# A recurrent (GRU) layer: q's high part made by ScalarE in the first two blocks, and the update gate's products all ahead of the candidate's

## The chip, the cores and the metric

The kernel runs on one core of one Trainium2 chip. The metric is the time of one execution on the device, in microseconds (us). Three runs of the kernel before gave 1056.73 us in the median, between 1056.33 and 1056.75.

## What is computed

64 sequences of 128 steps pass through a GRU with 512 inputs and 512 hidden units, all in float32. Every fourth step a further dense layer is put on the state that goes on:

```
z = sigmoid([x_t, h] @ Wz + bz)
r = sigmoid([x_t, h] @ Wr + br)
h_cand = tanh([x_t, r * h] @ Wh + bh)
h_new  = (1 - z) * h + z * h_cand
h_next = tanh(h_new @ Wp + bp) if (t + 1) % 4 == 0 and t < 127 else h_new
out[t] = x_t + h_new
```

In this document R, Z and C are the gates r, z and h_cand, and q is r * h, the operand of C's recurrent product.

## The kernel before

**Precision.** A float32 operand is held as two float16 parts, `hi` (the rounded value) and `lo` (what is left), both scaled. A product of two such operands is three matmuls: weights hi with values hi, weights lo with values hi, weights hi with values lo. The state and q lie in `h_split` and `q_split`, [128, 4, 2, 64]: four row groups of 128 hidden units, hi and lo, 64 sequences. HALVES are row groups 0 and 1 (LOW on TensorE) and 2 and 3 (HIGH).

**Products with x.** They do not depend on the state and are made ahead, in blocks of 8 steps: block 1's while block 0 runs, and so on. Block 1's are plain matmuls of 512 columns (`fill`); blocks 2 to 14 go by a scheme with seven products (`stage`, matmuls of 256 columns), for which the sums of weight quarters are made in steps 2 to 14 (`make_wsum`, `split_wsum`) and sums of x beside them (`make_x_sum`, `split_slot`). TensorE works on these between the end of one step's C product and the start of the next step's R product, so that it has work while gates and state are made.

**One step t, by engine** (every engine runs its own queue strictly in the order written; they meet in semaphores):

- TensorE: R's 48 recurrent matmuls of 64 columns, the first part of Z's among the last of them; the rest of Z's; then C's 48, which read `q_split`. The last four of Z's matmuls (row group 3, values lo) stand between C's matmuls on q's high part and those on its low part. Then come the products with x of this step.
- ScalarE: the sigmoid of R in two halves (`squash`, L504), the high part of a weight sum (L465) and of sums of x (L458) where the step has them, the sigmoid of Z, the tanh of C in two halves, and then the copies that put x's share into the accumulators (`seed`, L524) and bring the products with x out of PSUM.
- VectorE: per half `q_split` hi <- gate R * h (L868), then per half `q_full` <- gate R * h in float32 (L870), then per half q's low part <- `q_full` - hi (L857); the low parts of the sums (L714, L706); `keep` (L883), `new` (L888), the new state's hi part (L898), the full state (L901), its low part (L857), the output (L909), and then sums and maxima of x for later blocks.

Steps 0 to 15 are the first two blocks, BLOCK being 8. Weights are still being prepared in step 0 to 3 (`split_rec`, L692 and L498; magnitudes, L628).

Of the kernel before, what the change touches and what calls it, by code (L numbers as in the profile page):

```python
# [5 lines left out]
ALU = mybir.AluOpType  # L6
# [10 lines left out]
BLOCK = 8  # L17
RING = 4
R, Z, C, PROP = range(4)
# [40 lines left out]
def gru_kernel(nc, x, h0, wz, wr, wh, wp, biases, out):  # L60
# [106 lines left out]
    with ExitStack() as ctx:  # L167
# [150 lines left out]
        def propagates(t):  # L318
            return t % CHUNK == CHUNK - 1 and t < T - 1

        def props_before(t):
            return t // CHUNK

# [100 lines left out]
        def _(act):  # L424
# [75 lines left out]
            def squash(g, func, count, halves):  # L500

                act.wait_ge(product_done[g], count + 1)
                for half in halves:
                    nc.scalar.activation(gate[g][:, half, :], acc[g][:, half, :], func, scale=unscale[:, g:g + 1]).then_inc(gate_ready[g], 1)  # L504
# [70 lines left out]
            for t in range(T):  # L575
                m, s = divmod(t, BLOCK)
                first, middle, last = (n // PER_GROUP for n in fill_of(t))
                stages_first, stages_last = stages_of(t)
                wsum_gate, wsum_place = wsum_of(t)

                squash(R, ACT.Sigmoid, t, HALVES)
                if wsum_gate is not None:
                    split_wsum(wsum_gate, wsum_place)
                for block_m, slot in slots_at(t):
                    split_slot(block_m, slot)
                squash(Z, ACT.Sigmoid, t, WHOLE)
                squash(C, ACT.Tanh, t, HALVES)
                late = [g for g in (R, Z) if starts(t + 1) and groups_for(g, t + 1) > first]
                if t + 1 < T:
                    for g in (R, Z):  # L590
                        if g not in late:
                            seed(g, t + 1)
                if s in SPLIT_AT and m + 2 == LAST:
                    for k in SPLIT_AT[s]:
                        split_x(m + 2, k)
                if t == 2:
                    split_rec(PROP)
                    seed_prop(0)
                if propagates(t):
                    for n in range(first, middle):  # L600
                        copy_group(n)
                        seed_behind(n, late, t + 1)
                    for n in stages_first:
                        read_stage(m + 1, n)
                    squash(PROP, ACT.Tanh, props_before(t), HALVES)
                    for n in range(middle, last):
                        copy_group(n)
                        seed_behind(n, late, t + 1)
                    for n in stages_last:
                        read_stage(m + 1, n)  # L610
                    if props_before(t) + 1 < T // CHUNK - 1:
                        seed_prop(props_before(t) + 1)
                else:
                    for n in range(first, last):
                        copy_group(n)
                        seed_behind(n, late, t + 1)
                    for n in stages_last:
                        read_stage(m + 1, n)
                if t + 1 < T:
                    seed(C, t + 1)  # L620

        @block.vector
        def _(dve):
# [235 lines left out]
            for t in range(T):  # L859
# [2 lines left out]
                h_in = h_prop if t % CHUNK == 0 else h_even_odd[(t - 1) % 2]  # L862
                h_out = h_even_odd[t % 2]

                for n, half in enumerate(HALVES):

                    dve.wait_ge(gate_ready[R], 2 * t + n + 1)
                    nc.vector.tensor_tensor(q_split[:, half, 0, :], gate[R][:, half, :], h_in[:, half, :], ALU.mult).then_inc(q_hi_ready, 1)  # L868
                for half in HALVES:
                    nc.vector.tensor_tensor(q_full[:, half, :], gate[R][:, half, :], h_in[:, half, :], ALU.mult).then_inc(q_full_ready, 1)  # L870
                for n, half in enumerate(HALVES):
                    dve.wait_ge(q_hi_ready, 2 * t + n + 1)
# [75 lines left out]
        def _(pe):  # L948
# [169 lines left out]
            def rec(g, weights, values, k_of, lo):  # L1118

                for k in k_of:  # L1120
                    for j in range(KC):
                        mm = nc.tensor.matmul(acc[g][:, j, :], weights[g][:, k, j * P:(j + 1) * P], values[:, k, lo, :],  # L1122
                                              start=False, stop=False, skip_group_check=True)
                return mm
# [3 lines left out]
            for t in range(T):  # L1128
                m, s = divmod(t, BLOCK)
                first, middle, last = fill_of(t)  # L1130
                stages_first, stages_last = stages_of(t)

                if t == 0:
                    pe.wait_ge(wrec_hi_ready[R], 1)
                    pe.wait_ge(wrec_lo_ready[R], 1)
                pe.wait_ge(seed_ready[R], t + 1)
                pe.wait_ge(h_hi_ready, 2 * t + 1)
                rec(R, wrec_lo, h_split, LOW, 0)
                rec(R, wrec_hi, h_split, LOW, 0)
                pe.wait_ge(h_hi_ready, 2 * t + 2)  # L1140
                rec(R, wrec_lo, h_split, HIGH, 0)
                rec(R, wrec_hi, h_split, HIGH, 0)
                pe.wait_ge(h_lo_ready, 2 * t + 1)
                rec(R, wrec_hi, h_split, LOW, 1)
                if t == 0:
                    pe.wait_ge(wrec_hi_ready[Z], 1)
                    pe.wait_ge(wrec_lo_ready[Z], 1)
                pe.wait_ge(seed_ready[Z], t + 1)
                rec(Z, wrec_lo, h_split, LOW, 0)
                pe.wait_ge(h_lo_ready, 2 * t + 2)  # L1150
                rec(R, wrec_hi, h_split, HIGH, 1).then_inc(product_done[R], 1)

                rec(Z, wrec_hi, h_split, LOW, 0)
                rec(Z, wrec_lo, h_split, HIGH, 0)
                rec(Z, wrec_hi, h_split, HIGH, 0)
                rec(Z, wrec_hi, h_split, LOW, 1)
                rec(Z, wrec_hi, h_split, HIGH[:1], 1)

                if t == 0:
                    pe.wait_ge(wrec_hi_ready[C], 1)  # L1160
                    pe.wait_ge(wrec_lo_ready[C], 1)
                pe.wait_ge(seed_ready[C], t + 1)
                pe.wait_ge(q_hi_ready, 2 * t + 1)
                rec(C, wrec_lo, q_split, LOW, 0)
                rec(C, wrec_hi, q_split, LOW, 0)
                pe.wait_ge(q_hi_ready, 2 * t + 2)
                rec(C, wrec_lo, q_split, HIGH, 0)
                rec(C, wrec_hi, q_split, HIGH, 0)
                rec(Z, wrec_hi, h_split, HIGH[1:], 1).then_inc(product_done[Z], 1)
                pe.wait_ge(q_lo_ready, 2 * t + 1)  # L1170
                rec(C, wrec_hi, q_split, LOW, 1)
                pe.wait_ge(q_lo_ready, 2 * t + 2)
                rec(C, wrec_hi, q_split, HIGH, 1).then_inc(product_done[C], 1)

                if t == 1:
                    reduce_magnitude(PROP)
                if m + 2 < BLOCKS and s == scale_at(m + 2):
                    reduce_x_magnitude(m + 2)
                if propagates(t):
                    props = props_before(t)  # L1180
                    fill(first, middle)
                    for n in stages_first:
                        stage(m + 1, n)
                    if props == 0:
                        pe.wait_ge(wrec_hi_ready[PROP], 2)
                        pe.wait_ge(wrec_lo_ready[PROP], 2)
                    if m + 2 < BLOCKS and s > scale_at(m + 2):
                        pe.wait_ge(x_pow2_ready, 2 * (m + 3))
                    pe.wait_ge(seed_ready[PROP], props + 1)
                    pe.wait_ge(p_hi_ready, 2 * props + 1)  # L1190
                    rec(PROP, wrec_lo, p_split, LOW, 0)
                    rec(PROP, wrec_hi, p_split, LOW, 0)
                    pe.wait_ge(p_hi_ready, 2 * props + 2)
                    rec(PROP, wrec_lo, p_split, HIGH, 0)
                    rec(PROP, wrec_hi, p_split, HIGH, 0)
                    pe.wait_ge(p_lo_ready, 2 * props + 1)
                    rec(PROP, wrec_hi, p_split, LOW, 1)
                    pe.wait_ge(p_lo_ready, 2 * props + 2)
                    rec(PROP, wrec_hi, p_split, HIGH, 1).then_inc(product_done[PROP], 1)
                    fill(middle, last)  # L1200
                else:
                    fill(first, last)
                for n in stages_last:
                    stage(m + 1, n)
# [25 lines left out]
```

## Time and profile before

| | us |
|---|---|
| median of three runs | 1056.73 |
| the profiled execution | 1056.31 |
| its span, first to last instruction | 1054.5 |
| TensorE busy | 1044.9 (99%) |
| VectorE busy | 799.2 (76%) |
| ScalarE busy | 689.4 (65%) |

The span is 1.8 us shorter than the execution that it was taken from. A matmul's busy time counts from its start until its result is out, and matmuls overlap: one of 64 columns is shown as 0.19 us long while the next may start 0.03 us after it. So a short wait of TensorE shows in the distance between two starts and not as idle time. The granted clock was 2.4 GHz for all but the first microseconds (mean 0.999 of full speed).

### The profile page before, as it was taken

What the parts mean: (1) busy time and instruction counts of PE and PEld (TensorE: products, weight loads), DVE (VectorE), ACT (ScalarE), POOL (GpSimd) and SP (SyncE); (2) the same over time, 40 slices, a digit from 0 to 9 for tenths busy, and PEclk for the clock granted to TensorE, in tenths of its full rate; (3) what the DMA queues carried; (4) which work ended last, traced back from release to release, by engine and by line L of the source; (5) the groups of instructions that cost most, each with busy time, mean ns of one, the idle gap of its engine ahead of it and who ended that gap; (6) DMA issues with size and microseconds to landing.
All of it is one profiled execution on the core that took longest, in us unless ns stands there. A gap on an engine that the chain in (4) does not pass through costs nothing.

```text
span 1054.5 us, 53898 instructions
## 1 busy us (share of the span) xinstructions
PE 1044.9 (99%) x23984; PEld 966.2 (92%) x23984; DVE 799.2 (76%) x2692; ACT 689.4 (65%) x1666; POOL 0.2 (0%) x4
## 2 busy tenths in 40 slices
PE   9999999999999999999999999999999999999997
PEld 3477999999999999999999999999999999999997
DVE  6989988877777777777777777777777776666665
ACT  4766767666666666666666666666675666565664
POOL 0000000000000000000000000000000000000000
PEclk9999999999999999999999999999999999999999
DMA  9312211101111001111001110011110000000001
GB/s 325 110 43 83 77 59 43 44 3 44 43 43 44 23 23 44 43 43 43 21 26 43 44 43 22 24 43 43 43 43 23 24 23 24 23 24 23 24 4 43
DMA packets 38344, 47.63 MB, mean 45 GB/s; under 512 B 2144, under 2 KB 33760, under 8 KB 37728
## 3 DMA queue, kind: packets, MB, share of 16 engines
q1 hardware_dynamic: 38112, 44.19, 12.4%
q8 instruction: 188, 3.08, 1.2%
q14 instruction: 44, 0.36, 0.1%
HBM read 27.40 MB, written 16.78 MB: 42 GB/s over the span
## 4 chain that ended last, share of the span: by engine, by line
PE 94%; DVE 4%; ACT 1%; DMA 1%; issue 1%; SPq 0%; DVEq 0%
PE acc L1122 54%; PE x_acc L1047 34%; PE x_acc L953 5%; PE x_acc L1072 1%; DVE mag L628 1%; DMA x_blk<-x_dram 1%; DVE wrec_lo L692 1%; DVE mag_x L631 0%; DVE win_lo L684 0%; ACT gate L504 0%; DVE x_lo L699 0%; ACT wrec_hi L498 0%; DVE x_lo L706 0%; DVE keep L883 0%; DVE x_blk L909 0%
## 5 line engine op out<-in xcount | busy, mean ns | idle before, releaser
L504 ACT ACTIVATE gate<-acc,unscale 128x128 f32<-128x128 f32 x702 | 239.0, 384 | 268.7 <-PE acc L1122 268.4
L1122 PE MATMUL acc<-h_split,wrec_hi 128*128 128x64 f16 x8192 | 343.8, 193 | 0.0
L1047 PE MATMUL x_acc<-x_hi,win_hi 128*128 128x256 f16 x1092 | 297.7, 273 | 0.0
L1047 PE MATMUL x_acc<-x_hi,win_lo 128*128 128x256 f16 x1092 | 297.6, 273 | 0.0
L1047 PE MATMUL x_acc<-x_lo,win_hi 128*128 128x256 f16 x1092 | 297.6, 273 | 0.0
L1122 PEld LDWEIGHTS acc<-h_split,wrec_hi 128*128 128x128 f16 x8192 | 283.1, 98 | 0.0
L1122 PE MATMUL acc<-q_split,wrec_hi 128*128 128x64 f16 x5088 | 215.5, 193 | 0.0
L1122 PE MATMUL acc<-h_split,wrec_lo 128*128 128x64 f16 x4096 | 203.2, 193 | 1.4 <-DVE h_split L898 1.4
L470 ACT ACTIVATE x_part<-x_acc,bias,part_unscale 128x256 f32<-128x256 f32 x312 | 159.0, 561 | 47.5 <-PE x_acc L1047 47.4
L1122 PEld LDWEIGHTS acc<-q_split,wrec_hi 128*128 128x128 f16 x5088 | 179.2, 98 | 0.0
L524 ACT ACTIVATE acc<-x_part,seed_scale 128x256 f32<-128x256 f32 x384 | 172.7, 477 | 0.1
L1122 PEld LDWEIGHTS acc<-h_split,wrec_lo 128*128 128x128 f16 x4096 | 163.0, 98 | 6.2 <-ACT acc L524 1.5
L1122 PE MATMUL acc<-q_split,wrec_lo 128*128 128x64 f16 x2544 | 126.1, 193 | 1.4 <-DVE q_split L868 1.2
L1047 PEld LDWEIGHTS x_acc<-x_hi,win_lo 128*128 128x128 f16 x1092 | 106.8, 98 | 12.4
L1047 PEld LDWEIGHTS x_acc<-x_hi,win_hi 128*128 128x128 f16 x1092 | 106.8, 98 | 11.0
L1047 PEld LDWEIGHTS x_acc<-x_lo,win_hi 128*128 128x128 f16 x1092 | 106.8, 98 | 10.9
L1122 PEld LDWEIGHTS acc<-q_split,wrec_lo 128*128 128x128 f16 x2544 | 98.0, 98 | 3.3 <-issue 2.6
L868 DVE TENSOR_TENSOR q_split<-gate,h_even 128x128 f16<-128x128 f32 x128 | 35.1, 292 | 73.4 <-ACT gate L504 73.3
L779 DVE SCALAR_TENSOR_TENSOR x_part<-x_acc,part_unscale,x_part 128x512 f32<-128x512 f32 x78 | 58.3, 749 | 30.8 <-ACT x_part L470 15.2
L888 DVE SCALAR_TENSOR_TENSOR new<-gate,scale 128x128 f32<-128x128 f32 x256 | 78.5, 348 | 0.0
L857 DVE TENSOR_TENSOR q_split<-q_full,q_split 128x128 f16<-128x128 f32 x256 | 62.3, 284 | 0.3 <-issue 0.3
L953 PE MATMUL x_acc<-x_lo,win_hi 128*128 128x128 f16 (+2 forms) x224 | 59.9, 288 | 0.0
(116 smaller groups left out, 1059.8 us busy)
## 6 DMA issues: line engine op xcount, KB each, us to landing
out_dram<-x_blk SPq DMA_DIRECT2D x30, 512.0 KB, 3.2
x_blk<-x_dram SPq DMA_DIRECT2D x24, 512.0 KB, 4.2
x_blk<-x_dram SPq DMA_DIRECT2D x3, 1024.0 KB, 8.8
x_blk<-x_dram SPq DMA_DIRECT2D x4, 256.0 KB, 4.0
x_part<-wz_dram SPq DMA_DIRECT2D x4, 256.0 KB, 7.0
x_part<-wh_dram SPq DMA_DIRECT2D x4, 256.0 KB, 6.6
x_part<-wr_dram SPq DMA_DIRECT2D x1, 1024.0 KB, 11.1
x_part<-wz_dram SPq DMA_DIRECT2D x1, 1024.0 KB, 13.3
```

Of the source, the lines that this page charges most:

```text
L470: nc.scalar.activation(part_quarter(m, g, jh, nh)[:, j], in_halves(x_acc[bank][:])[:, j], ACT.Identity, bias=bias[:, g, 2 * jh + j:2 * jh ...
L504: nc.scalar.activation(gate[g][:, half, :], acc[g][:, half, :], func, scale=unscale[:, g:g + 1]).then_inc(gate_ready[g], 1)
L524: nc.scalar.activation(acc[g], added, ACT.Copy, scale=seed_scale[:, g:g + 1]).then_inc(seed_ready[g], 1)
L628: nc.vector.tensor_reduce(mag[:, col:col + 1], src, AX_X, ALU.max, apply_absolute_value=True).then_inc(mag_ready[col], 1)
L692: nc.vector.scalar_tensor_tensor(out=flat(wrec_lo[g][:, rows]), in0=flat(stage_rec[g][:, rows]), scalar=scale[:, g:g + 1], in1=flat(wrec_h ...
L779: nc.vector.scalar_tensor_tensor(out=part_quarter(m, g, jh, 1), in0=in_halves(x_acc[bank][:]), scalar=part_unscale[:, m % 2, g:g + 1], in1 ...
L857: return nc.vector.tensor_tensor(split[:, half, 1, :], full[:, half, :], split[:, half, 0, :], ALU.subtract)
L868: nc.vector.tensor_tensor(q_split[:, half, 0, :], gate[R][:, half, :], h_in[:, half, :], ALU.mult).then_inc(q_hi_ready, 1)
L888: nc.vector.scalar_tensor_tensor(out=new[:, half, :], in0=gate[C][:, half, :], scalar=h_scale, in1=gate[Z][:, half, :], op0=ALU.mult, op1= ...
L953: return nc.tensor.matmul(x_acc[bank][:, 0:cols], weights[g][:, 2 * (j // 2) + k // 2, k % 2, j % 2 * P:(j % 2 + 1) * P], values[m % 2][:, ...
L1047: mm = nc.tensor.matmul(in_halves(x_acc[bank][:])[:, j], weights[g][:, slot_w, k, j * P:(j + 1) * P], in_halves(values[m % 2][:, slot_x, : ...
L1122: mm = nc.tensor.matmul(acc[g][:, j, :], weights[g][:, k, j * P:(j + 1) * P], values[:, k, lo, :], start=False, stop=False, skip_group_che ...
```

## The change

For steps below 16 (`high_by_act`), VectorE no longer computes q's high part. It makes the two halves of `q_full`, each as soon as the half of gate R is there, and ScalarE copies each half of `q_full` into the high part of `q_split`, converting to float16. The copies stand in ScalarE's queue behind R's sigmoid and ahead of the step's other work. VectorE's subtraction for the low part waits for the copy, as it waited for its own product before. In the same steps TensorE issues Z's last four matmuls ahead of C's first. From step 16 on everything is as before.

```diff
+        def high_by_act(t):
+
+            return t < 2 * BLOCK
...
                 squash(R, ACT.Sigmoid, t, HALVES)
+                if high_by_act(t):
+                    for n, half in enumerate(HALVES):
+                        act.wait_ge(q_full_ready, 2 * t + n + 1)
+                        nc.scalar.copy(q_split[:, half, 0, :], q_full[:, half, :]).then_inc(q_hi_ready, 1)
                 if wsum_gate is not None:
                     split_wsum(wsum_gate, wsum_place)
...
+                if not high_by_act(t):
+                    for n, half in enumerate(HALVES):
+                        dve.wait_ge(gate_ready[R], 2 * t + n + 1)
+                        nc.vector.tensor_tensor(q_split[:, half, 0, :], gate[R][:, half, :], h_in[:, half, :], ALU.mult).then_inc(q_hi_ready, 1)
                 for n, half in enumerate(HALVES):
-
                     dve.wait_ge(gate_ready[R], 2 * t + n + 1)
-                    nc.vector.tensor_tensor(q_split[:, half, 0, :], gate[R][:, half, :], h_in[:, half, :], ALU.mult).then_inc(q_hi_ready, 1)
-                for half in HALVES:
                     nc.vector.tensor_tensor(q_full[:, half, :], gate[R][:, half, :], h_in[:, half, :], ALU.mult).then_inc(q_full_ready, 1)
...
                 rec(Z, wrec_hi, h_split, HIGH[:1], 1)
 
+                behind = not high_by_act(t)
+                if not behind:
+                    rec(Z, wrec_hi, h_split, HIGH[1:], 1).then_inc(product_done[Z], 1)
+
...
                 rec(C, wrec_hi, q_split, HIGH, 0)
-                rec(Z, wrec_hi, h_split, HIGH[1:], 1).then_inc(product_done[Z], 1)
+                if behind:
+                    rec(Z, wrec_hi, h_split, HIGH[1:], 1).then_inc(product_done[Z], 1)
                 pe.wait_ge(q_lo_ready, 2 * t + 1)
```

TensorE's queue in step 0 before, from Z's last matmuls to C's last:

```order
L1122 MATMUL acc<-h_split,wrec_hi 128x64 x20
L1122 MATMUL acc<-q_split,wrec_lo 128x64 [waits seed_ready2,q_hi_ready,wrec_lo_ready2,wrec_hi_ready2]
L1122 MATMUL acc<-q_split,wrec_lo 128x64 x7
L1122 MATMUL acc<-q_split,wrec_hi 128x64 x8
L1122 MATMUL acc<-q_split,wrec_lo 128x64 [waits q_hi_ready]
L1122 MATMUL acc<-q_split,wrec_lo 128x64 x7
L1122 MATMUL acc<-q_split,wrec_hi 128x64 x8
L1122 MATMUL acc<-h_split,wrec_hi 128x64 x4
L1122 MATMUL acc<-q_split,wrec_hi 128x64 [waits q_lo_ready]
```

And the same place in the changed kernel:

```order
L1131 MATMUL acc<-h_split,wrec_hi 128x64 x24
L1131 MATMUL acc<-q_split,wrec_lo 128x64 [waits seed_ready2,q_hi_ready,wrec_lo_ready2,wrec_hi_ready2]
L1131 MATMUL acc<-q_split,wrec_lo 128x64 x7
L1131 MATMUL acc<-q_split,wrec_hi 128x64 x8
L1131 MATMUL acc<-q_split,wrec_lo 128x64 [waits q_hi_ready]
L1131 MATMUL acc<-q_split,wrec_lo 128x64 x7
L1131 MATMUL acc<-q_split,wrec_hi 128x64 x8
L1131 MATMUL acc<-q_split,wrec_hi 128x64 [waits q_lo_ready]
```

The four Z matmuls have moved from behind 32 of C's to ahead of all of them; the number of matmuls is the same.

ScalarE's queue in step 2 before, from the second half of R's sigmoid to the tanh of C:

```order
L504 ACTIVATE gate<-acc,unscale 128x128
L465 ACTIVATE win_hi<-sum_b,scale 128x512 [waits wsum_made]
L504 ACTIVATE gate<-acc,unscale 128x256 [waits product_done1]
L504 ACTIVATE gate<-acc,unscale 128x128 [waits product_done2]
L504 ACTIVATE gate<-acc,unscale 128x128
```

And the same place in the changed kernel:

```order
L508 ACTIVATE gate<-acc,unscale 128x128
L589 CAST q_split<-q_full 128x2x64 [waits q_full_ready] x2
L469 ACTIVATE win_hi<-sum_b,scale 128x512 [waits wsum_made]
L508 ACTIVATE gate<-acc,unscale 128x256 [waits product_done1]
L508 ACTIVATE gate<-acc,unscale 128x128 [waits product_done2]
L508 ACTIVATE gate<-acc,unscale 128x128
```

Two instructions of a form (CAST) that ScalarE did not have before now stand between R's sigmoid and the rest of the step, and each waits for VectorE.

## Rows read from the trace of the kernel before

**Rows 1.** The page, chain that ended last, by engine, shares of the span.

```profile
PE 94%; DVE 4%; ACT 1%; DMA 1%; issue 1%; SPq 0%; DVEq 0%
```

**Rows 2.** TensorE's waits: who waited <- for whom: us in total, times, longest.

```profile
PE acc L1122 <- DVE q_split L868: 1.2, 3, 0.5
```

**Rows 3.** Timeline, step 13: start us, us, engine, line, operation, tiles, how many.

```profile
152.30 0.63 ACT L504 ACTIVATE gate<-acc,unscale 128x128 f32<-128x128 f32 x2 [2.87 <-PE acc L1122]
...
152.33 0.40 PE L1122 MATMUL acc<-h_split,wrec_lo 128*128 128x64 f16 x8
...
152.56 0.75 PE L1122 MATMUL acc<-h_split,wrec_hi 128*128 128x64 f16 x20
...
152.70 0.55 DVE L868 TENSOR_TENSOR q_split<-gate,h_even 128x128 f16<-128x128 f32 x2 [1.04 <-ACT gate L504]
...
152.82 0.72 ACT L465 ACTIVATE win_hi<-sum_b,scale 128x512 f16<-128x512 f32 x1
...
153.15 0.40 PE L1122 MATMUL acc<-q_split,wrec_lo 128*128 128x64 f16 x8
...
154.40 1.09 ACT L504 ACTIVATE gate<-acc,unscale 128x256 f32<-128x256 f32 x3 [0.25 <-PE acc L1122]
```

**Rows 4.** Timeline, step 3: TensorE and VectorE at the start of C's product.

```profile
74.26 0.75 PE L1122 MATMUL acc<-h_split,wrec_hi 128*128 128x64 f16 x20
...
75.02 0.54 DVE L868 TENSOR_TENSOR q_split<-gate,h_even 128x128 f16<-128x128 f32 x2 [0.21 <-ACT gate L504]
...
75.45 0.22 PE L1122 MATMUL acc<-q_split,wrec_lo 128*128 128x64 f16 x2 [0.45 <-DVE q_split L868]
```

**Rows 5.** Groups by line and shape: busy us, mean ns of one, idle before.

```profile
L443 ACT ACTIVATE x_part<-x_acc,bias,part_unscale 128x512 f32<-128x512 f32 x20 | 14.9, 773 | 13.0 <-PE x_acc L953 13.0
...
L443 ACT ACTIVATE x_part<-x_acc,bias 128x512 f32<-128x512 f32 x4 | 2.4, 674 | 0.0
...
L483 ACT COPY x_acc<-x_acc 128x512 f32<-128x512 f32 x39 | 22.2, 569 | 16.2 <-PE x_acc L1047 16.0
...
L465 ACT ACTIVATE win_hi<-sum_b,scale 128x512 f16<-128x512 f32 x6 | 4.3, 718 | 0.0
...
L498 ACT ACTIVATE wrec_hi<-x_blk,scale 128x1024 f16<-128x1024 f32 x2 | 2.2, 1142 | 0.0
...
L543 ACT ACTIVATE warm<-warm 128x1 f32<-128x1 f32 x1 | 0.2, 203 | 0.0
...
L868 DVE TENSOR_TENSOR q_split<-gate,h_even 128x128 f16<-128x128 f32 x128 | 35.1, 292 | 73.4 <-ACT gate L504 73.3
...
L870 DVE TENSOR_TENSOR q_full<-gate,h_even 128x128 f32<-128x128 f32 x128 | 31.1, 284 | 0.0
```

**Rows 6.** Timeline, at 42 us: ScalarE is released by VectorE.

```profile
42.40 0.15 DVE L654 TENSOR_SCALAR scale<-inv_pow 128x1 f32<-128x1 f32 x1
...
42.59 2.00 ACT L498 ACTIVATE wrec_hi<-x_part,scale 128x2048 f16<-128x2048 f32 x1 [0.91 <-DVE scale L654]
```

**Rows 7.** Timeline, step 6 up to step 7's R product: VectorE, TensorE and ScalarE.

```profile
97.22 0.48 DVE L868 TENSOR_TENSOR q_split<-gate,h_odd 128x128 f16<-128x128 f32 x2
...
98.43 0.74 DVE L714 SCALAR_TENSOR_TENSOR win_lo<-sum_c,scale,win_hi 128x512 f16<-128x512 f32 x1
...
100.42 0.41 DVE L883 SCALAR_TENSOR_TENSOR keep<-gate,h_odd 128x256 f32<-128x256 f32 x1
...
101.28 0.48 DVE L898 TENSOR_TENSOR h_split<-new,keep 128x128 f16<-128x128 f32 x2
...
101.75 0.40 PE L1122 MATMUL acc<-h_split,wrec_lo 128*128 128x64 f16 x8
```

**Rows 8.** Timeline, step 7: TensorE and VectorE at the start of C's product.

```profile
103.85 0.75 PE L1122 MATMUL acc<-h_split,wrec_hi 128*128 128x64 f16 x20
...
104.09 0.68 DVE L631 TENSOR_REDUCE mag_x<-x_blk 128x1 bf16<-128x512 f32 x1
...
104.69 0.48 DVE L868 TENSOR_TENSOR q_split<-gate,h_even 128x128 f16<-128x128 f32 x2
...
105.11 0.28 PE L1122 MATMUL acc<-q_split,wrec_lo 128*128 128x64 f16 x4 [0.52 <-DVE q_split L868]
```

## Prediction, on record before the changed kernel ran

> **What bounds the kernel now.** I read four views. First the chain that ended last: TensorE holds 94% of it [rows 1], so the time is TensorE's work plus its waits. Next TensorE's own waits: it is charged 1.2 us in three places for q's high part, the part that the change touches [rows 2]. That is too little, since a matmul is drawn 0.19 us long while it holds the array far shorter, so I then read the timeline for distances between starts. In step 13 eight matmuls take from 152.33 to 152.56, 0.029 us each [rows 3]. The 20 Z matmuls that start at 152.56 are therefore issued by 153.14, and C's first starts at 153.15: no wait. In step 3 the same 20 end at 74.84 and C starts at 75.45, a gap of 0.61 us; in step 7 it is 104.43 against 105.11, 0.68 us [rows 4, 8]. Read in the same way, the 16 steps that the change touches fall in two sorts: nine without a gap (4, 5, 8 to 11, 13 to 15; I call them clean), and seven late ones, with gaps of 0.38, 0.10, 0.17, 0.61, 0.06, 0.68 and 0.06 us in steps 0, 1, 2, 3, 6, 7 and 12, 2.06 us together. Rows of one clean and two late steps stand for all. Last, the groups by shape, for the price of what is added [rows 5].
>
> **How tight a clean step is.** In late steps the time from the start of q's first high half to C's first matmul is the handoff itself: 75.02 to 75.45, and 104.69 to 105.11, so 0.43 and 0.42 [rows 4, 8]. In step 13 the half starts at 152.70; with 0.43 it is usable at 153.13, and TensorE comes for it at 153.14 to 153.15 [rows 3]. The spare is 0.02 us. So anything that makes q's high part later is paid by TensorE at once, in all 16 steps.
>
> **Part 1, q's high part goes through ScalarE.** VectorE makes `q_full` where it made the high part: same operands, 284 ns against 292, which I take as the same [rows 5]. Behind it come a handoff to ScalarE and one CAST of 128 elements per partition, D. The handoff: VectorE's `scale` ends at 42.40 + 0.15 = 42.55 and the waiting ScalarE starts at 42.59, 0.04 us [rows 6]. The handoff from ScalarE to TensorE I take as that from VectorE, already in the 0.43.
>
> D does not occur in the trace. The upper bound is the same kind of copy with a scale operand, SBUF to SBUF: 718 ns at 512 elements and 1142 at 1024, so 0.83 ns an element, and 718 - 384 x 0.83 = 400 ns at 128 [rows 5]. The lower bound is ScalarE's plain COPY, 569 ns at 512, whose source is PSUM: 250 ns at 128 [rows 5]. Between: L443 takes 773 ns with a scale operand, 674 without, and COPY without any 569, so each such operand costs about 0.10 us; without its one, the 400 become 300. The one-element ACTIVATE, 203 ns, plus 127 x 0.83 gives 309 [rows 5]. I take 0.30 us. There is no room for a D near nothing: even one element takes 0.20.
>
> The Trainium skill puts a price on the same thing and speaks against the edit ("VectorE: DVE Perf Modes", section on the TRN2 errata, SBUF-src ops): a ScalarE operation that reads SBUF costs 224 cycles plus one per element at 1.2 GHz, because its latency is exposed once per instruction. By that D would be an estimated 0.29 us and the sum below 3.3 us; by the COPY row alone it would be 2.65. No row here shows the instruction itself.
>
> ScalarE is free in time: its second R half starts 0.27 us behind the first at 152.30 and it goes on at 152.82 [rows 3], while the first copy can start only at 152.70 + 0.29 + 0.04 = 153.03. The second half follows 0.2 us behind, and C's matmuls want it 16 x 0.029 = 0.47 us after the first: covered. The low parts are wanted 32 x 0.029 = 0.93 us after C's start, and need one subtraction and a handoff after the copy (0.28 + 0.18): covered too.
>
> **Part 2, four Z matmuls move ahead of C.** Work is unchanged. They give 4 x 0.029 = 0.117 us more cover ahead of C, and shorten the stretch from C's start to its end by as much. Z's sigmoid can run sooner, but in step 13 Z (0.47 of the 1.09 us row) and the tanh fit behind one another without delaying the tanh [rows 3], so nothing comes of that.
>
> **Sum per step.** Late: handoff + D - cover = 0.04 + 0.30 - 0.12 = 0.22 us. Clean: less the spare, 0.20 us. Five late steps (0 to 3, 12): 1.1 us. Nine clean: 1.8 us.
>
> **Steps 6 and 7** need their own working, because there VectorE has no idle time at all from the low part of step 6 to q of step 7. VectorE loses two instructions a step (about 0.2 us each from start to start), but its subtraction now waits for ScalarE's copy, and behind it are queued the low parts of the weight sum and of x's sums, `keep`, `new` and the state. Counted from q's start at 97.22: copies start at 0.32 and 0.52, ScalarE gets to the weight sum at 0.73, done at 1.45, so VectorE's part of it starts at 1.49 where it started at 1.21 [rows 7]; `keep` comes at 3.47 instead of 3.20. In step 5 the same leaves VectorE about 0.06 later against TensorE. The state's high part, 101.28 + 0.43 = 101.71, is 0.04 us ahead of R's start at 101.75 [rows 7]. Step 6: 0.06 + 0.22 = 0.28. R of step 7: 0.27 + 0.06 - 0.04 - 0.28, about 0.01. Step 7: 0.04 of backlog that comes through the unbroken row of sums and maxima [rows 8] + 0.22 = 0.26. Together 0.55. Steps 5 and 8 to 15 have more room: 0.1 us or more ahead of the next R by the same count, which the sum does not use up.
>
> Total: 1.1 + 1.8 + 0.55 = 3.45 us. Against the profiled execution, 1056.31 us (span 1054.5 and 1.8 around it), that is 1059.8; it lies 0.4 under the median of the runs, 1056.73, from which I forecast **1060.2 us**, 0.33% slower. With D at 0.25 the sum is 16 x 0.05 less, 2.65 us, 1059.4. With D at 0.40 it is 1.6 more, and steps 6 to 9, with ScalarE later again, some 0.3 on top: 5.3 us, 1062.0.
>
> **Rivals.**
> *VectorE's relief pays for the late steps.* Two of its instructions go per step, 0.4 us. If what makes q late in the seven late steps is the saved work itself, their gaps (2.06 us) go, all 16 steps cost 0.20, and 3.2 - 2.06 = 1.1 us is left: 1057.8 us, no measurable change. It decides in step 7, whose gap of 0.68 is two reliefs wide, and from the point where VectorE's low part no longer waits for the copy. For it: VectorE runs without a break there [rows 7, 8]. Against it: the wait for the copy takes the relief back, and in step 3 VectorE itself idled 0.21 us for ScalarE [rows 4]; in steps 0 to 2 the late work stands behind the previous C, where nothing was saved.
> *ScalarE's queue backs up.* In steps with a weight sum and two sums of x it has about 1.8 us between R's and Z's sigmoid. If its copies cost more start to start than 0.2 us, Z's sigmoid, the tanh and then the state are late, and R of steps 6, 7 and 9 waits. Price: 0.2 to 0.4 us in each of about five steps on top of the sum, 4.8 us, 1061.5. For: 0.04 us of room before R of step 7 [rows 7]. Against: in step 13 ScalarE idled 0.25 us for Z even behind two such copies [rows 3].
> *The change does not do what it says* cannot be: the order of the queues shows both moves.
>
> **How the numbers follow.** The forecast has 0.74, the relief 0.12, the backed-up queue 0.10, and 0.04 is for a gain from a source that I don't see. A measurement here tells about 0.2%, 2.1 us, from no change. For the forecast to fall under that D would have to be 0.22 or less; I move 0.05 of it there. So: faster 0.04, same 0.17, slower 0.79. The range, 1058.8 to 1062.0, takes in D from 0.25 to 0.40 and the backed-up queue, and leaves the relief out.
>
> **What the profile of the changed kernel would show.** CAST rows of ScalarE near 0.30 us, starting 0.04 after `q_full`'s end. C's first matmul 0.77 us after `q_full`'s start, and a gap of 0.20 us behind the 24 Z matmuls in clean steps; in step 3 one of about 0.83. The weight sum's low part about 0.3 us later than before. From step 16 on the two traces should run in parallel. CAST rows of 0.2 us or less, or a step 7 gap below 0.5, would prove me wrong.

## Result: 1059.66 us, 0.3% slower

| | kernel before | changed kernel |
|---|---|---|
| median, us | 1056.39 (9 runs, 1056.10 to 1057.37) | 1059.66 (9 runs, 1059.33 to 1060.10) |
| ratio, 95% interval | | 1.003 (1.002 to 1.004) |
| the profiled execution, us | 1056.31 | 1060.1 |
| its span, us | 1054.5 | 1058.3 |

The change costs 3.27 us; 3.45 was forecast. As a time that was 1060.2 us, since the forecast started from a median of 1056.73 where the one beside the changed kernel is 1056.39. All executions of every kernel lie within 1.1 us of its median except one of experiment 12, which took 2153.11 us and is left out.

The profiled execution is 3.8 us longer than that of before, but 0.46 of it lies ahead of anything that was changed: the first recurrent matmul of step 0 starts at 51.14 us before and at 51.60 after, and over all profiles of this case that start moves between 50.9 and 51.9. From there to the last matmul the changed kernel takes 3.34 us more. TensorE's clock plays no part: in both traces the granted clock is 2.4 GHz from 10 us on until the last matmul. In the kernel before it falls again only behind the last matmul (0.67 of full speed from 1052.0 to 1054.5).

TensorE's waits in the changed kernel (who waited <- for whom: us in total, times, longest):

```profile
PE acc L1131 <- ACT q_split L589: 2.3, 5, 0.8
```

It answers to [rows 2]: the releaser is now ScalarE's copy on line 589, and as before the view shows only the part of a gap that is longer than a matmul is drawn.

The same step 13 as in [rows 3], from the timeline (start us, us, engine, line, operation, tiles, how many):

```profile
155.61 0.62 ACT L508 ACTIVATE gate<-acc,unscale 128x128 f32<-128x128 f32 x2 [2.86 <-PE acc L1131]
...
155.87 0.86 PE L1131 MATMUL acc<-h_split,wrec_hi 128*128 128x64 f16 x24
...
156.01 0.55 DVE L879 TENSOR_TENSOR q_full<-gate,h_even 128x128 f32<-128x128 f32 x2 [0.98 <-ACT gate L508]
...
156.33 0.56 ACT L589 CAST q_split<-q_full 128x128 f16<-128x128 f32 x2
...
156.77 0.39 PE L1131 MATMUL acc<-q_split,wrec_lo 128*128 128x64 f16 x8
...
157.55 0.75 DVE L722 SCALAR_TENSOR_TENSOR win_lo<-sum_b,scale,win_hi 128x512 f16<-128x512 f32 x1 [0.33 <-ACT win_hi L469]
```

The 24 Z matmuls are issued by 155.87 + 24 x 0.029 = 156.57 and C starts at 156.77: a gap of 0.20 us where there was none. From `q_full`'s start to C it is 0.76 us: 0.29 for `q_full`, 0.03 of handoff, 0.30 for the copy, 0.14 to TensorE. VectorE's low part of the weight sum comes 1.54 us after `q_full`'s start, with 0.33 us of idling for ScalarE ahead of it. Before, it came 1.27 us after the start of q (152.70), without idling:

```profile
153.97 0.75 DVE L714 SCALAR_TENSOR_TENSOR win_lo<-sum_b,scale,win_hi 128x512 f16<-128x512 f32 x1
```

The two late steps of [rows 4] and [rows 8], TensorE alone, step 3 and step 7:

```profile
75.36 0.86 PE L1131 MATMUL acc<-h_split,wrec_hi 128*128 128x64 f16 x24
76.89 0.22 PE L1131 MATMUL acc<-q_split,wrec_lo 128*128 128x64 f16 x2 [0.67 <-ACT q_split L589]
...
105.87 0.86 PE L1131 MATMUL acc<-h_split,wrec_hi 128*128 128x64 f16 x24
107.51 0.28 PE L1131 MATMUL acc<-q_split,wrec_lo 128*128 128x64 f16 x4 [0.78 <-ACT q_split L589]
```

With 0.70 us for the 24, the gaps are 0.83 and 0.94 us; they were 0.61 and 0.68. The price of one copy, from the groups by shape:

```profile
L589 ACT CAST q_split<-q_full 128x128 f16<-128x128 f32 x32 | 8.6, 298 | 3.1 <-DVE q_full L879 2.0
```

Read in this way, TensorE's gaps in the first eight steps are (us; "layer" is the extra layer's product, whose operand is the new state; "R of 7" the start of step 7's R product; beside them five of the next section's experiments, by number):

| gap at | before | changed | exp. 1 | exp. 2 | exp. 5 | exp. 7 | exp. 8 |
|---|---|---|---|---|---|---|---|
| C of 0 | 0.38 | 0.59 | 0.71 | 0.26 | 0.69 | 0.37 | 0.26 |
| C of 1 | 0.09 | 0.31 | 0.42 | 0 | 0.41 | 0.30 | 0 |
| C of 2 | 0.17 | 0.38 | 0.50 | 0.05 | 0.48 | 0.37 | 0.05 |
| C of 3 | 0.61 | 0.83 | 0.94 | 0.49 | 0.93 | 0.83 | 0.50 |
| layer, 3 | 0.27 | 0.27 | 0.27 | 0.27 | 0.27 | 0.49 | 0.27 |
| C of 4 | 0 | 0.21 | 0.32 | 0 | 0.31 | 0 | 0 |
| C of 5 | 0 | 0.21 | 0.32 | 0 | 0.31 | 0.20 | 0 |
| C of 6 | 0.06 | 0.34 | 0.34 | 0 | 0.47 | 0.29 | 0.21 |
| R of 7 | 0 | 0.02 | 0 | 0 | 0.09 | 0.23 | 0.35 |
| C of 7 | 0.68 | 0.94 | 0.99 | 0.61 | 1.04 | 0.72 | 0.61 |
| layer, 7 | 0.27 | 0.27 | 0.27 | 0.27 | 0.27 | 0.49 | 0.32 |

In steps 8 to 15 the changed kernel has 0.20 to 0.21 us in each, 0.28 in step 12.

### The profile page after: what moved, and what is told of

Same layout as the page of the kernel before. It is cut to its first block, busy times and chain, and to the rows that moved or that the text cites. A ratio compares the mean times of both kernels' runs of the same rounds, so it can differ in the third digit from the quotient of the medians.

```text
span 1058.3 us, 53898 instructions
## 1 busy us (share of the span) xinstructions
PE 1047.4 (99%) x23984; PEld 967.4 (91%) x23984; DVE 796.8 (75%) x2660; ACT 696.1 (66%) x1698; POOL 0.2 (0%) x4
## 4 chain that ended last, share of the span: by engine, by line
PE 93%; DVE 5%; ACT 1%; issue 1%; DVEq 0%; ACTq 0%
PE acc L1131 53%; PE x_acc L1056 34%; PE x_acc L962 4%; PE x_acc L1081 1%; DVE mag L636 1%; DVE wrec_lo L700 1%; DVE mag_x L639 0%; ACT gate L508 0%; DVE h_split L907 0%; DVE x_blk L918 0%; DVE win_lo L692 0%; DVE new L897 0%; ACT q_split L589 0%; DVE x_lo L707 0%; ACT wrec_hi L502 0%
## 5 line engine op out<-in xcount | busy, mean ns | idle before, releaser
L876 DVE TENSOR_TENSOR q_split<-gate,h_even 128x128 f16<-128x128 f32 x112 | 30.9, 293 | 70.3 <-ACT gate L508 70.3
L962 PE MATMUL x_acc<-x_hi,win_hi 128*128 128x128 f16 (+2 forms) x224 | 59.9, 288 | 0.0
```

What stands on the lines that cost most here:

```text
L962: return nc.tensor.matmul(x_acc[bank][:, 0:cols], weights[g][:, 2 * (j // 2) + k // 2, k % 2, j % 2 * P:(j % 2 + 1) * P], values[m % 2][:, ...
```

## The experiments

All comparisons are with the kernel before, run on the same chip; the twelve kernels fall into four groups, whose medians of before were 1056.44, 1056.38, 1056.38 and 1056.51 us.

**1. The copy without the Z move.** Line numbers aside, one line of the changed kernel:

```diff
-                behind = not high_by_act(t)
+                behind = True
```

> The changed kernel with Z's last four matmuls back behind C's high parts; ScalarE still makes q's high part in steps 0 to 15. If the cover ahead of C counts to the nanosecond: C starts at the same moment after q_full, its stretch is 4 x 0.029 = 0.117 us longer, in 16 steps 1.9 us over the changed kernel, 1061.5 us, 5.1 us over the kernel before; gap in clean steps 0.32 us. If the place of the four matmuls is worth nothing (something else sets C's start): as the changed kernel, 1059.7.

Measured: 1061.31 us, ratio 1.0046 (1.0034 to 1.0059), 4.9 us over before. In step 13:

```profile
156.43 0.75 PE L1131 MATMUL acc<-h_split,wrec_hi 128*128 128x64 f16 x20
157.33 0.39 PE L1131 MATMUL acc<-q_split,wrec_lo 128*128 128x64 f16 x8 [0.16 <-ACT q_split L589]
```

The 20 end at 157.01, the gap is 0.32 us. The four matmuls are worth their 0.117 us in clean steps, and in steps 0 to 3 too; in steps 6 and 7 (table) less comes of them, which is the 0.2 us by which the sum was too high.

**2. The Z move without the copy, in steps 0 to 15.**

```diff
-            return t < 2 * BLOCK
+            return False
...
-                behind = not high_by_act(t)
+                behind = t >= 2 * BLOCK
```

> The kernel before with Z's last four matmuls ahead of C in steps 0 to 15; VectorE makes q's high part as before. If cover is what counts: each late step gets back the smaller of its gap and 0.117 us, in steps 0, 1, 2, 3, 6, 7 and 12 together 0.68 us, clean steps nothing: 1055.7 against 1056.4. If Z's order is neutral: 1056.4.

Measured: 1055.76 us, 0.68 under before, ratio 0.9995 (0.9986 to 1.0003): alone not told from no change, but the gaps of its profile (table) are nearly those expected: those of steps 0, 2 and 3 are 0.12 less, those of 1, 6 and 12 are gone, and only step 7's falls by 0.07 where 0.117 was expected. Together that is 0.65 us for the 0.68. Step 3, whose gap was 0.61 and is 75.35 - 74.16 - 0.70 = 0.49:

```profile
74.16 0.86 PE L1131 MATMUL acc<-h_split,wrec_hi 128*128 128x64 f16 x24
75.35 0.39 PE L1131 MATMUL acc<-q_split,wrec_lo 128*128 128x64 f16 x8 [0.33 <-DVE q_split L876]
```

**3. The Z move in all 128 steps.** `behind = False`, VectorE makes the high part everywhere.

> As the last one, in all 128 steps. From step 16 on the trace of before has 26 steps with a gap of about 0.06 us at C's start, 1.63 us together, all under 0.117. Cover theory: 0.68 + 1.63 = 2.3 us faster than before, 1054.1. Neutral order: 1056.4.

Measured: 1054.20 us, ratio 0.998 (0.9972 to 0.9989), 2.24 us faster, and no gap is left at C from step 16 on. The two halves of the change are worth opposite things, and they are not independent. The order of Z gains 0.7 us by itself (2.2 if done everywhere) and 1.6 beside the copy; the copy costs 4.9 us by itself and 3.9 with Z's matmuls moved.

**4. The whole change in the seven late steps alone.**

```diff
-            return t < 2 * BLOCK
+            return t in (0, 1, 2, 3, 6, 7, 12)
```

> The whole change in the seven late steps alone (0 to 3, 6, 7, 12). My sum: 0.22 us in each of the first four, 12 and 6, and about 0.25 in step 7 with the next R: 1.6 us over before, 1058.0. If VectorE's relief paid for late steps, their gaps of 2.06 us would shrink: 1056.4 or below.

Measured: 1058.28 us, ratio 1.0016 (1.0007 to 1.0025), 1.84 over before. So the rival by which VectorE's relief pays for the late steps falls: they pay as the others do. Its profile holds one wait of VectorE on itself that the changed kernel's lacks, in step 7:

```profile
109.96 0.49 DVE L907 TENSOR_TENSOR q_split<-new,keep 128x128 f16<-128x128 f32 x2 [0.20 <-DVE new L897]
```

With it the extra layer's product waits 0.56 us in place of 0.27, and that accounts for the 0.24 us over the sum's 1.6. The last section says where such waits stand.

**5. A dearer copy.** The copy as an ACTIVATE with a scale operand, a column of ones:

```diff
-                        nc.scalar.copy(q_split[:, half, 0, :], q_full[:, half, :]).then_inc(q_hi_ready, 1)
+                        nc.scalar.activation(q_split[:, half, 0, :], q_full[:, half, :], ACT.Copy, scale=unity[:]).then_inc(q_hi_ready, 1)
```

> The changed kernel with the copy as an ACTIVATE that takes a scale operand (of ones), which the rows of before put at 0.40 us in place of 0.30. If D is paid in full in every step: 16 x 0.10 = 1.6 us and up to 0.3 for ScalarE's later queue, 1061.3 to 1061.6. If D is partly hidden: under 1060.5.

Measured: 1061.68 us, ratio 1.0049 (1.0035 to 1.0063), 2.0 over the changed kernel by the differences to before (5.30 against 3.27).

```profile
L590 ACT ACTIVATE q_split<-q_full,unity 128x128 f16<-128x128 f32 x32 | 11.1, 394 | 3.1 <-DVE q_full L881 2.0
```

394 ns against 298: 0.096 us more for each copy, and clean gaps of 0.31 in place of 0.21. Every step pays D in full: the gaps at C add up to 1.66 us more than in the changed kernel. R of step 7 waits 0.09 us in place of 0.02, the start of the backed-up queue. The four executions leave the median less sure than the gaps.

**6. The change in all 128 steps.** `high_by_act` returns True.

> The change in all 128 steps. Law of 0.205 us a step without and 0.215 with a gap: 3.3 + 86 x 0.205 + 26 x 0.215 = 26.5 us over before, 1082.9. If ScalarE's two more instructions back its queue up in the steps with four readings of stages, more than 1085; if VectorE's relief is worth something there, less than 1080.

Measured: 1082.36 us, ratio 1.0246 (1.0232 to 1.0260), 26.0 us over before, 0.5 under the law. Its gaps at C add up to 26.5 us more than those of before, as the law has it; where the other 0.5 came back I have not found. Neither a backed-up queue nor a relief shows in the 112 steps where ScalarE also reads the stages out. One of its later steps:

```profile
499.88 0.86 PE L1131 MATMUL acc<-h_split,wrec_hi 128*128 128x64 f16 x24
500.79 0.39 PE L1131 MATMUL acc<-q_split,wrec_lo 128*128 128x64 f16 x8
```

0.91 us less 0.70 leaves the same 0.21.

**7. Other work into the gap.** In the changed kernel, steps 0 to 7:

```diff
                 if not behind:
                     rec(Z, wrec_hi, h_split, HIGH[1:], 1).then_inc(product_done[Z], 1)
+                if t < BLOCK:
+                    fill(first, first + 1)
+                    first += 1
```

> The changed kernel, and in steps 0 to 7 one matmul with x (512 columns, 0.216 us) moved from behind C to between Z and C. It fills the gap; the question is whether the stretch behind C can spare it. By the chains behind C: yes in steps 0, 1, 2, 4 and 5 (1.05 us back), no in 3 and 7, where the products of the extra layer already wait 0.27 us for the state, nor in 6, where the next R waits: 1.05 us under the changed kernel, 1058.6. If cover is worth the same everywhere: 1.7 us, 1058.0. If not worth anything: 1059.7.

Measured: 1059.60 us, ratio 1.0032 (1.0019 to 1.0044): 3.22 over before where the changed kernel has 3.27. A miss by 1 us. In step 1:

```profile
60.35 0.86 PE L1131 MATMUL acc<-h_split,wrec_hi 128*128 128x64 f16 x24
61.05 0.38 PE L962 MATMUL x_acc<-x_hi,win_hi 128*128 128x512 f16 x1
61.57 0.39 PE L1131 MATMUL acc<-q_split,wrec_lo 128*128 128x64 f16 x8
...
58.62 2.28 DVE L636 TENSOR_REDUCE mag<-x_blk 128x1 bf16<-128x2048 f32 x1
60.81 0.48 DVE L879 TENSOR_TENSOR q_full<-gate,h_even 128x128 f32<-128x128 f32 x2
```

The inserted matmul fills 0.216 us, and behind it the gap is still 61.57 - 61.27 = 0.30, as in the changed kernel without it. VectorE runs from the 2.28 us maximum straight into q: the moment of q follows from the end of the C before, not from R. R came 0.216 us sooner, since one matmul less stood ahead of it, and q waited that much longer behind it: from the start of R's sigmoid to `q_full` it is 0.73 us here (60.08 to 60.81) and 0.51 in the changed kernel. In step 5 it is 0.62 against 0.40, behind a maximum of x. In steps 0, 4 and 7 the gap did shrink (table), but R of 7 and the two extra layers gave it back. I had priced the inserted matmul as cover; what counts in these steps is the length of the path from C over tanh and state through the work queued behind them on ScalarE and VectorE to the next q and C, and that had not become shorter. I call this path the loop.

**8. Only the second half by ScalarE.** VectorE makes the first half of the high part, then the second and the first half of `q_full`; Z ahead. VectorE's part of the edit is left out here.

```diff
-                    for n, half in enumerate(HALVES):
-                        act.wait_ge(q_full_ready, 2 * t + n + 1)
-                        nc.scalar.copy(q_split[:, half, 0, :], q_full[:, half, :]).then_inc(q_hi_ready, 1)
+                    act.wait_ge(q_full_ready, 2 * t + 1)
+                    act.wait_ge(q_hi_ready, 2 * t + 1)
+                    nc.scalar.copy(q_split[:, HALVES[1], 0, :], q_full[:, HALVES[1], :]).then_inc(q_hi_ready, 1)
```

> In steps 0 to 15 VectorE makes the first half of q's high part, ScalarE copies the second, Z ahead as in the changed kernel. The second half is wanted 0.47 us after the first: in clean steps the copy is ready at 1.66 us after R's last matmul and wanted at 1.66, no gap; in late ones it is about 0.07 late, of the 0.117 won. So 0.2 to 0.4 us under before, 1056.1. If any copy by ScalarE costs 0.2 us whichever half it is: 1059.7.

Measured: 1056.80 us, ratio 1.0004 (0.9995 to 1.0013), no change, where I had 0.2 to 0.4 us of gain. The half of the mechanism that was asked for holds: clean steps have no gap, so it is the first half's copy that costs, and a copy wanted 0.47 us later is free. What I had left out is behind it: VectorE still waits for ScalarE's weight sum, and since C is no longer late TensorE arrives before the state is there.

```profile
97.25 0.39 PE L1143 MATMUL acc<-q_split,wrec_lo 128*128 128x64 f16 x8
...
98.30 0.75 DVE L722 SCALAR_TENSOR_TENSOR win_lo<-sum_c,scale,win_hi 128x512 f16<-128x512 f32 x1 [0.19 <-ACT win_hi L469]
...
101.58 0.39 PE L1143 MATMUL acc<-h_split,wrec_lo 128*128 128x64 f16 x8 [0.18 <-DVE h_split L919]
```

These are steps 6 (a gap of 0.21 at C) and 7 (0.35 at R); R of step 9 waits another 0.14. The weight sum's low part comes 1.48 us after q's start in step 6, where it was 1.21 before and is 1.47 in the changed kernel: the same backlog, which the changed kernel's later C had hidden. The new order also makes VectorE idle 0.10 us for its own `q_full` in each of the 16 steps.

**9 and 10. One maximum of x later.** A quarter's maximum moves from step 6 to step 7, behind the state:

```diff
-SEVEN_MAG_AT = {2: (1, 1, 3, 3), 3: (-4, -3, -2, -1)}
+SEVEN_MAG_AT = {2: (1, 1, 3, 3), 3: (-4, -3, -1, -1)}
```

> Z's last four matmuls ahead of C in all 128 steps, q's high part by VectorE as before, and one maximum of x (0.60 us of VectorE from start to start) taken from step 6 to step 7, behind the state, where VectorE idles 0.99 us before step 8. If step 7's gap at C, 0.61 us with Z ahead, is VectorE's queue: it goes to about 0.01, and the time to 0.6 us under that of the Z order alone, 1053.6, 2.8 under before. If it comes from ScalarE or the next loads: no change, 1054.2.

Measured: 1053.54 us, ratio 0.9975 (0.9965 to 0.9984): 2.84 under before, against 2.24 for the Z order alone. Step 7:

```profile
103.39 0.86 PE L1131 MATMUL acc<-h_split,wrec_hi 128*128 128x64 f16 x24
104.11 0.39 PE L1131 MATMUL acc<-q_split,wrec_lo 128*128 128x64 f16 x8
```

A gap of 0.02 us where there were 0.61: it was VectorE's queue. This is the fastest kernel of the study and keeps nothing of the copy.

> The changed kernel with the same maximum of x taken from step 6 to step 7. If VectorE's queue sets step 7's gap, 0.94 us falls to about 0.34 and the time by 0.6 us, 1059.0; the 0.2 us of the copy stay. If ScalarE's queue sets it: 1059.6.

Measured: 1059.47 us, ratio 1.0028 (1.0017 to 1.0039), 3.09 over before, so 0.2 under the changed kernel and not 0.6. The gap of step 7 did fall, from 0.94 to 0.34, and the trace from the first recurrent matmul on is 0.51 us shorter. Its profile has a wait of VectorE on itself again, which gives 0.14 us back at the extra layer:

```profile
110.48 0.50 DVE L865 TENSOR_TENSOR q_split<-h_odd,q_split 128x128 f16<-128x128 f32 x2 [0.26 <-DVE h_odd L910]
```

The medians, each uncertain by about 1 us, do not settle the remaining 0.3.

**11 and 12. Who paces which steps.** In the kernel before, a matmul with x is done a second time, behind C, and its result overwritten by the first of the group, so only TensorE's work grows; ahead of late steps in the one, ahead of clean steps in the other. The second has `again = t in (4, 8, 10, 13)`.

```diff
+                    if again and c == 0:
+                        x_product(g, j, m, k, part, n % BANKS, steps, True)
                     mm = x_product(g, j, m, k, part, n % BANKS, steps)
...
+                again = t in (0, 1, 2, 5, 6)
```

> The kernel before, with one matmul with x (512 columns, 0.216 us) done twice, behind C of steps 0, 1, 2, 5 and 6, so 1.08 us more work for TensorE; the result is the same. The next steps' gaps at C are 0.09, 0.17, 0.61, 0.06 and 0.68 us. If those steps are paced by the loop through ScalarE and VectorE (q there is timed by the end of the C before, not by R), each gap swallows what it can: 0.13 + 0.05 + 0 + 0.16 + 0 = 0.33 us slower. If TensorE paces them: 1.08 us.

Measured: 1056.94 us, 0.43 over before, ratio 1.0003 (0.9994 to 1.0012), for 1.08 us of work. Step 3's gap has swallowed the 0.216:

```profile
74.92 0.75 PE L1125 MATMUL acc<-h_split,wrec_hi 128*128 128x64 f16 x20
75.89 0.19 PE L1125 MATMUL acc<-q_split,wrec_lo 128*128 128x64 f16 x1 [0.23 <-DVE q_split L868]
```

75.89 - 74.92 - 0.58 = 0.39 against 0.61; the gaps of steps 1, 2 and 6 are gone, that of 7 is 0.51 against 0.68. Together 0.71 us of the 1.08 is swallowed, and from the first recurrent matmul to step 16 the trace is 0.39 us longer.

> The kernel before, with one matmul with x done twice behind C of step 4 (512 columns) and five of 256 columns (0.109 us each) in steps 8, 10 and 13, 0.76 us more work ahead of steps without a gap. If TensorE paces those: 0.76 us slower. If the loop paces them too: 0.

Measured: 1057.16 us, the median of ten, 0.65 over before, ratio 1.0009 (1.0 to 1.0018), for 0.76 us of work. From the first recurrent matmul to step 16 the trace is 0.79 us longer, and of the gaps at C only step 7's is smaller, by 0.06. So the late steps of the first block are paced by the loop through ScalarE and VectorE, and the steps ahead of which this work was put by TensorE. This bears out the reading of experiment 7. The two intervals touch or include no change; what carries the reading is the gaps and the two lengths up to step 16.

## Why the prediction was right

**The spare of 0.02 us in clean steps** was right, and it carried the result. Experiment 6 shows it for steps 16 on as well.

**D and the handoffs.** 0.30 us estimated, 0.298 measured; handoff to ScalarE 0.04 against 0.03; the handoff from ScalarE to TensorE is, as assumed, that of VectorE. The step from COPY at 569 ns over 674 to 773, read as about 0.10 us for each operand read from memory, was the one that hit; experiment 5 confirms it from the other side, 0.394 for the estimated 0.40. The figure of the Trainium skill ("VectorE: DVE Perf Modes", section on the TRN2 errata), an estimated 0.29 us, agrees with the 0.298 too; the lower bound from the PSUM COPY row, 0.25, was too low; its source is PSUM, that of the copy SBUF.

**Sum per step.** Clean 0.20 forecast, 0.20 to 0.21 measured. Late 0.22 forecast; 0.22, 0.21, 0.21, 0.22 and 0.22 in steps 0 to 3 and 12. Step 6: 0.28 forecast, 0.29 measured. R of step 7: 0.01 against 0.02. Step 7: 0.26 against 0.26. The gaps at C from step 0 to 15 and at R of step 7 add up to 3.5 us more than before, as the sum has it. From the first to the last recurrent matmul the profile has 3.34, and the medians 3.27. The difference is mostly one wait that nobody forecast: in step 15 of the kernel before, the first product with x starts 0.13 us late, behind a VectorE queue that had idled 0.16 us (row in the last section), and the changed kernel has no such wait there. That 0.13 us is luck.

**The queue behind VectorE's wait** was right in kind and size: the weight sum's low part moved from 1.27 to 1.54 us behind q's start, where about 0.3 was forecast.

**The rivals.** The relief fell with experiment 4 (1.84 us slower, where it gave none). The backed-up queue did not come at D = 0.30; at 0.39 its first 0.09 us show in experiment 5.

**What was not right behind it.** The prediction called the four Z matmuls "cover". In clean steps that is the same as their price, and so the sum came out. In the late steps behind another C the gain has another cause, which the prediction names in the same sentence but does not use: C's own stretch is 0.117 us shorter, and with it the loop. The evidence is the pair of experiments 2 and 7: moving 0.117 us out of C's stretch took it off the gaps of steps 2 and 3 (and all 0.09 of step 1's), moving 0.216 us from behind C to ahead of it left the gaps of steps 1, 2 and 3 as they were. In step 0, with no C before it, both moves shrank the gap, so there it was cover. My expectation for experiment 7 built on the wrong word and missed by 1 us.

## What to carry to other kernels

Before moving a step of a dependent chain to an idle engine, subtract when its result is usable from when the consumer comes for it: here the spare was 0.02 us, and the second engine in the chain cost its instruction plus a handoff, 0.33 us, and relieving the first engine paid none of it back. The half that the consumer wants later can be moved without that price, but count what is queued on both engines behind the new wait. And where the loop through the small engines paces a stretch, filling TensorE's gap with other work gains nothing; only taking work out of the loop does.

## What the runs showed of the hardware

A CAST on ScalarE of 128 float32 elements per partition to float16, SBUF to SBUF, took 298 ns; as an ACTIVATE with a scale operand 394 ns. The second CAST of a step starts 0.20 us after the first where its operand comes 0.20 us later, and otherwise 0.26, again with its operand.

Not expected: VectorE at times idles 0.16 to 0.27 us ahead of an instruction that waits for nothing but VectorE's own results. In step 7 only experiments 4 and 10 have this (0.20 and 0.26 us, at two different instructions), but every profile has three to eight such places behind the first recurrent matmul. The kernel before has one in step 15:

```profile
172.36 0.29 DVE L857 TENSOR_TENSOR q_split<-h_odd,q_split 128x128 f16<-128x128 f32 x1 [0.16 <-issue]
```

If VectorE's records in the trace are numbered from 0, with its semaphore waits among them, all 80 such places of the 14 profiles have a number that is 63 or 64 above a multiple of 128: 576 for this row, 319 for those of experiments 4 and 10. So they go with the place in VectorE's instruction stream, not with the time or with the instruction. The change takes two instructions of VectorE out of each of 16 steps and so moves all later ones. The DMA part of the page of before has a queue that brings instructions (packets, MB, share of 16 engines):

```profile
q14 instruction: 44, 0.36, 0.1%
```

Behind the start of each of the 80 instructions that had idled so, a packet of 8192 bytes starts in this queue within 0.6 to 1.4 us. That points to the loading of VectorE's instructions, 128 at a time, but no experiment here tested it.
